# Cross-attention in two layers on one core: constants written into PSUM ahead of the products, g spread by a block transpose and two transfers, new orders on the engines

## What is computed

```python
# layer 0                                      # layer 1, on the x of layer 0
Q = x @ Wq + bq; K = c @ Wk + bk               q = x @ Wq + bq; k = c @ Wk + bk
V = c @ Wv + bv                                v = c @ Wv + bv
weights = softmax(Q @ K.T * scale, axis=-1)    w = softmax(q @ k.T * scale, axis=1)   # over the queries
x = x + (weights @ V) @ Wo + bo                y = w @ v + x
                                               y = (y - mean) * rsqrt(var + eps) * gamma + beta
```

## Time and profile before

| | |
|---|---|
| median of 3 runs | 1249.71 us (1248.47 to 1250.39) |
| the profiled execution's own time | 1247.58 us |
| its span, first to last instruction | 1245.8 us |
| busy PE | 1206.5 us, 97% |
| busy DVE | 892.8 us, 72% |
| busy ACT | 699.2 us, 56% |
| busy POOL | 926.9 us, 74% |
| the transfer engines' mean busy share | 5 to 6 tenths in most slices |
| mean granted TensorE clock | 0.989 of 2.4 GHz |

### The profile page before, as it was taken

One profiled execution on the slowest core, in us unless ns is written; L12 is line 12 of the kernel. 1 busy time (PEld: TensorE's weight loads), 2 busy tenths in 40 slices (PEclk: granted clock), 3 DMA queues, 4 the chain that ended last, 5 costly groups with the idle time before them and its releaser, 6 DMA issues.

```text
span 1245.8 us, 25385 instructions
## 1 busy us (share of the span) xinstructions
PE 1206.5 (97%) x8304; PEld 1116.0 (90%) x8304; DVE 892.8 (72%) x1874; ACT 699.2 (56%) x1545; POOL 926.9 (74%) x713
## 2 busy tenths in 40 slices
PE   6989999999999999999999999999999999999984
PEld 5779999999999999999999999999999999999973
DVE  1447777777777777777777777777777777777763
ACT  2436556555656655565665556565555656555542
POOL 2436778778777877887787788778778877877764
PEclk8999999999999999999999999999999999999998
DMA  8346556656656655665666566566656655665431
GB/s 329 104 142 210 175 201 222 196 188 210 227 168 207 222 195 185 219 219 170 206 222 195 184 216 221 175 202 220 197 182 219 219 180 199 219 196 186 153 119 51
DMA packets 121727, 241.36 MB, mean 194 GB/s; under 512 B 13920, under 2 KB 79456, under 8 KB 113120
## 3 DMA queue, kind: packets, MB, share of 16 engines
q1 hardware_dynamic: 120816, 240.18, 58.0%
q10 hardware_dynamic: 880, 0.79, 0.2%
HBM read 157.03 MB, written 83.89 MB: 193 GB/s over the span
## 4 chain that ended last, share of the span: by engine, by line
PE 92%; POOL 2%; DMA 2%; DVE 1%; issue 1%; ACT 1%; ACTq 0%; POOLq 0%; SPq 0%; DVEq 0%
PE bank L275 85%; PE bank L392 2%; PE bank L365 2%; DMA beta_b<-in_beta 1%; PE bank L344 1%; PE bank L402 1%; PE bank L408 1%; POOL PT_lo L915 0%; POOL Y L963 0%; DVE stats L802 0%; POOL yT_lo L915 0%; POOL Y L966 0%; PE bank L421 0%; ACT Y L603 0%; POOL rstd L953 0%
## 5 line engine op out<-in xcount | busy, mean ns | idle before, releaser
L915 POOL TENSOR_TENSOR PT_lo<-PT_raw,PT_hi 128x512 fp32r<-128x512 f32 x64 | 82.6, 1291 | 192.6 <-ACT PT_hi L482 192.6
L603 ACT ACTIVATE Y<-R,nmr,rstd 128x512 f32<-128x512 f32 x128 | 97.5, 809 | 184.5 <-POOL nmr L955 184.5
L915 POOL TENSOR_TENSOR xT_lo<-IN,xT_hi 128x1024 fp32r<-128x1024 f32 x64 | 154.2, 2409 | 24.7 <-ACT xT_hi L482 24.7
L915 POOL TENSOR_TENSOR yT_lo<-yT_raw,yT_hi 128x1024 fp32r<-128x1024 f32 x64 | 154.1, 2407 | 21.4 <-ACT yT_hi L482 21.4
L963 POOL TENSOR_TENSOR Y<-Y,gamma_b 128x512 f32<-128x512 f32 x128 | 162.8, 1294 | 3.7 <-ACT Y L603 3.7
L966 POOL TENSOR_TENSOR Y<-Y,beta_b 128x512 f32<-128x512 f32 x128 | 163.4, 1299 | 0.0
L275 PE MATMUL bank<-yT_hi,A_hi 128*128 128x256 f32 x512 | 144.5, 282 | 4.9 <-POOL yT_lo L915 4.9
L275 PE MATMUL bank<-yT_lo,A_hi 128*128 128x256 f32 x512 | 144.9, 283 | 0.0
L275 PE MATMUL bank<-yT_hi,A_lo 128*128 128x256 f32 x512 | 144.7, 283 | 0.0
L275 PE MATMUL bank<-xT_hi,A_hi 128*128 128x256 f32 x512 | 144.1, 281 | 0.0
L275 PE MATMUL bank<-xT_lo,A_hi 128*128 128x256 f32 x512 | 144.0, 281 | 0.0
(11 more groups left out here) (116 smaller groups left out, 4199.0 us busy)
## 6 DMA issues: line engine op xcount, KB each, us to landing
IN<-in_packed SPq DMA_DIRECT2D x64, 1024.0 KB, 5.7
R<-in_x SPq DMA_DIRECT2D x64, 512.0 KB, 6.3
y_dram<-y_blk SPq DMA_DIRECT2D x256, 128.0 KB, 2.4
yT_raw<-y_dram SPq DMA_DIRECT2D x64, 512.0 KB, 3.6
out<-Y SPq DMA_DIRECT2D x64, 512.0 KB, 3.5
E_dram<-E_blk SPq DMA_DIRECT2D x256, 64.0 KB, 1.8
PT_raw<-E_dram SPq DMA_DIRECT2D x64, 256.0 KB, 2.7
WqT_s<-in_WqT SPq DMA_DIRECT2D x2, 1024.0 KB, 11.5
```

The lines of the kernel that those rows point to most:

```text
L603: nc.scalar.activation(Y[n.k % 2][:, q, :], R[n.k % 4][:, q, :], ACT.Identity, bias=nmr[:, q:q + 1], scale=rstd[:, q:q + 1]).then_inc(Y_se ...
L915: return nc.gpsimd.tensor_tensor(dst, src, fp(hi), ALU.subtract)
```

## The change

What the changed kernel does:

- **out.** `out_seed_` on ACT writes c1 * Z0 into the bank before the products of `out_`, which then add to it (`seeded=True`: no matmul starts a new sum). c1 is a row made in the setup from bo and bv. The banks of `out_` and of `pred_` are no longer the same.
- **S1 and g.** `g_` and `gT_` are gone. `dot` writes g into the first column of a block of 32, `g_blocks` on DVE transposes the blocks, SP writes 256 numbers to DRAM (`write_g`) and reads them back to all 128 partitions (`read_g`), `S1_seed_` on ACT copies them into the bank of S1, and the products add to it. The addition on DVE is gone.
- **s.** `w_low_sum` on DVE adds the two halves of w_lo; `s_` is 3 matmuls with a tile of ones. `s_h` and `s_l` are gone. `s_columns` on DVE brings s into columns by four transposes, each on 32 partitions, 64 numbers a partition. s shares its bank with u, so `u_` of the next body waits for `s_columns`.
- **pred.** `pred_seed_` on DVE writes bv*s + x1 into the bank; the two bias matmuls and `x2` are gone. `moments` and `normalise` read the bank.
- **Orders.** The bodies of all five engines have new orders, and the setup of PE, ACT, DVE and SP too. In it one matmul with the tile of ones is new, and POOL's constants are gone.

```diff
-        g_bank = s_bank = bank[0]
+        out_bank = (bank[0], bank[3])
         Pc_bank = v_bank = bank[1]
-        u_bank = bank[2]
-        g1_b = bank[3]
+        u_bank = s_bank = bank[2]
         S0_bank = wc_bank = bank[4]
         S1_bank = bank[5]
-        out_bank = pred_bank = bank[6:8]
+        pred_bank = bank[6:8]
...
-                first(sp, Y_set, n.count(2, 1, back=4))
+                first(sp, pred_seed, n.count(2, 1, back=4))
...
+            def write_g(n):
+                if not n.there():
+                    return
+                sp.wait_ge(g_blk_set, n.count())
+                sp.dma_start(g_dram.rearrange("q i t -> i q t"), g_blk[0:P:32, :, :]).then_inc(g_out, 16)
+            def read_g(n):
+                if not n.there():
+                    return
+                sp.wait_ge(g_out, n.count(16, 15))
+                sp.dma_start(gT[:, 0, :], g_dram.rearrange("(a q) i t -> a (q i t)", a=1).to_broadcast([P, S])
+                             ).then_inc(g_in, 16)
...
             def body(r):
+                write_g(r.plus(1))
+                load_x(r.plus(2))
                 load_IN(r.plus(5))
-                load_x(r.plus(2))
-                store(r.plus(-2))
+                read_g(r.plus(1))
                 move_E0(r.plus(3))
                 move_y(r.plus(2))
+                store(r.plus(-2))
...
-            def product(dst, stat, mov, k, first=True):
+            def product(dst, stat, mov, k, seeded=False):
                 for t in range(k):
                     for n, (a, b) in enumerate(((0, 0), (0, 1), (1, 0))):
-                        last = nc.tensor.matmul(dst, stat(a, t), mov(b, t), start=(first and t == 0 and n == 0),
-                                                stop=(t == k - 1 and n == 2))
+                        last = nc.tensor.matmul(dst, stat(a, t), mov(b, t), start=(not seeded and t == 0 and n == 0),
+                                                stop=(t == k - 1 and n == 2), skip_group_check=seeded)
                 return last
...
+                first(pe, s_set, n.count(back=4))
...
-                first(pe, x1_set, n.count(2, q, back=1))
-                first(pe, x2_set, n.count(2, q, back=3))
+                pe.wait_ge(out_seed, n.count(2, q))
                 product(out_bank[q][:, :], lambda a, t: PcT[a][:, t, q * P:(q + 1) * P],
-                        lambda b, t: Bv[b][:, t, :], LT).then_inc(out_full, 1)
+                        lambda b, t: Bv[b][:, t, :], LT, seeded=True).then_inc(out_full, 1)
...
-            def g_(n):
-                if not n.there():
-                    return
-                pe.wait_ge(g_set, n.count(2, 1))
-                first(pe, s_lo, n.count(back=1))
-                for q in range(ST):
-                    last = nc.tensor.transpose(g_bank[:, q * P:(q + 1) * P],
-                                               gcol[n.k % 2][:, q:q + 1].to_broadcast([P, P]), ident[:, :])
-                last.then_inc(g_full, 1)
-
             def S1_(n):
                 if not n.there():
                     return
                 pe.wait_ge(v_lo, n.count())
-                first(pe, w_lo, n.count(back=1))
+                pe.wait_ge(S1_seed, n.count())
                 for m in range(ST):
                     last = product(cols(S1_bank, m), lambda a, t: cTs[n.k % 4][a][:, t, m * P:(m + 1) * P],
-                                   lambda b, t: vT[b][:, t, :], LT)
+                                   lambda b, t: vT[b][:, t, :], LT, seeded=True)
                 last.then_inc(S1_full, 1)
             def s_(n):
                 if not n.there():
                     return
-                pe.wait_ge(w_lo, n.count())
-                pe.wait_ge(gT_set, n.count())
-                for t in range(ST):
-                    for b in range(2):
-                        last = nc.tensor.matmul(s_bank[:, 0:S], pick[:, :], w[b][:, t, :],
-                                                start=(t == 0 and b == 0), stop=(t == ST - 1 and b == 1))
+                if n.plus(3).there():
+                    pe.wait_ge(u_lo, n.plus(3).count(2, 1))
+                else:
+                    pe.wait_ge(s_set, n.count(back=1))
+                pe.wait_ge(w_los_set, n.count())
+                for t, part in enumerate((w[0][:, 0, :], w[0][:, 1, :], w_los[:, :])):
+                    last = nc.tensor.matmul(s_bank[:, 0:S], ones[:, :], part, start=(t == 0), stop=(t == 2))
                 last.then_inc(s_full, 1)
...
-                    pe.wait_ge(s_lo, n.count())
                     pe.wait_ge(wc_lo, n.count())
-                if n.plus(2).there():
-                    pe.wait_ge(x1_set, n.plus(2).count(2, q))
-                else:
-                    pe.wait_ge(x2_set, n.count(2, q, back=1))
-                dst = pred_bank[q][:, :]
-                nc.tensor.matmul(dst, srow[:, q * P:(q + 1) * P], bvK[:, :], start=True, stop=False)
-                product(dst, lambda a, t: wcT[a][:, t, q * P:(q + 1) * P], lambda b, t: V1[b][:, t, :], LT,
-                        first=False).then_inc(pred_full, 1)
+                pe.wait_ge(pred_seed, n.count(2, q))
+                product(pred_bank[q][:, :], lambda a, t: wcT[a][:, t, q * P:(q + 1) * P],
+                        lambda b, t: V1[b][:, t, :], LT, seeded=True).then_inc(pred_full, 1)
...
+            over_h(bank[7][:, :], wide(1), Wo0_s)
...
+            pe.wait_ge(su_lo, 7)
+            A_half(bank[5], WqT1_s, WkT1_s, 1)
...
-            over_h(bank[5][:, :], wide(1), Wo0_s)
+            pe.wait_ge(su_lo, 9)
+            pe.wait_ge(ones_set, 2)
+            nc.tensor.matmul(S1_bank[:, :], ones[:, :], Bv[0][:, 0, :], start=True, stop=True).then_inc(su_full, 1)
             v_(Seq(0))
-            pe.wait_ge(const_set, 2)
-            pe.wait_ge(pick_set, 2)
-            pe.wait_ge(su_lo, 11)
             def body(r, u=True):
                 if u:
                     u_(r.plus(3))
+                S1_(r)
                 Pc_(r.plus(2))
-                g_(r)
-                S1_(r)
                 S0_(r.plus(3))
                 pred_(r.plus(-1), 0)
                 pred_(r.plus(-1), 1)
...
-            def gT_(n):
-                if not n.there():
-                    return
-                act.wait_ge(g_full, n.count())
-                first(act, S1_sum, n.count(back=1))
-                copy(gT[:, 0, :], g_bank[:, 0:S]).then_inc(gT_set, 1)
+            def S1_seed_(n):
+                if not n.there():
+                    return
+                act.wait_ge(g_in, n.count(16, 15))
+                first(act, w_lo, n.count(back=1))
+                copy(S1_bank[:, :].rearrange("p (a b) -> p a b", a=ST), gT[:, :, :].to_broadcast([P, ST, S])
+                     ).then_inc(S1_seed, 1)
+            def out_seed_(n):
+                if not n.there():
+                    return
+                act.wait_ge(E0_set, n.count())
+                for q in range(ST):
+                    first(act, x1_set, n.count(2, q, back=1))
+                    copy(out_bank[q][:, :], c1_b[:, :], scale=Z0[:, q:q + 1]).then_inc(out_seed, 1)
...
-            def s_h(n):
-                if not n.there():
-                    return
-                act.wait_ge(s_full, n.count())
-                first(act, pred_full, n.count(2, 1, back=1))
-                copy(srow[0:96, :], s_bank[0:96, 0:S]).then_inc(s_hi, 1)
-
...
-                    nc.scalar.activation(Y[n.k % 2][:, q, :], R[n.k % 4][:, q, :], ACT.Identity,
+                    nc.scalar.activation(Y[n.k % 2][:, q, :], pred_bank[q][:, :], ACT.Identity,
...
             def body(r, prefix=True):
                 if prefix:
                     wc_h(r.plus(-1))
+                    u_h(r.plus(3))
                     C_h(r.plus(3))
-                    u_h(r.plus(3))
+                xT_h(r.plus(4))
+                if prefix:
+                    out_seed_(r.plus(2))
+                exps1(r)
                 Pc_h(r.plus(2))
-                gT_(r)
+                w_h(r)
                 yT_h(r.plus(1))
+                exps0(r.plus(3))
+                S1_seed_(r.plus(1))
+                v_h(r.plus(1))
                 cT_h(r.plus(4))
-                xT_h(r.plus(4))
-                exps0(r.plus(3))
-                exps1(r)
-                w_h(r)
                 normalise(r.plus(-1))
-                v_h(r.plus(1))
-                s_h(r)
                 PT_h(r.plus(3))
...
-                first(dve, g_set, n.count(2, q, back=1))
-                first(dve, g_full, n.count(back=2))
                 nc.vector.scalar_tensor_tensor(junk[q][:, :], R[n.k % 4][:, q, :], 1.0, g1_b[:, :], ALU.mult,
-                                               ALU.mult, accum_out=gcol[n.k % 2][:, q:q + 1]).then_inc(g_set, 1)
+                                               ALU.mult, accum_out=gcol[:, q, 0:1]).then_inc(g_set, 1)
+            def g_blocks(n):
+                if not n.there():
+                    return
```

(77 more changed lines are left out.)

110 lines of the change are left out of this document (49 added, 61 removed).

## The result

The changed kernel takes 1400.7 us (median of 4 runs, 1400.3 to 1401.1), the kernel before 1249.6 (4 runs): a ratio of 1.121, 95% interval 1.1195 to 1.1224. I had forecast 1245, range 1203 to 1264. The profiled execution took 1400.27 us, its span is 1398.5.

The account below looks back on a forecast made before the run. PE bound the kernel before at 18.15 us a body; after, a loop through s_columns of 10.62 + 7.46 = 18.08 would, gaining 4.2 us. With setup +4 and tail -3.9 that is -4.1 from 1249.7: about 1245, range 1203 to 1264.

Parts of the forecast that it names:

- All totals remain below 17.3.: Busy totals of ACT, DVE and POOL per body after the change: all stay below 17.3 us.
- New is w_low_sum: ... like srow's 0.42 less the overlap, 0.34.: DVE leg of the loop: the new sum of the w_lo halves, 256 columns, priced at 0.34 us.
- the walk: Loop from u's first matmul through ACT, DVE and s_columns back to u: 10.62 + 7.46 = 18.08 us a round.
- The ends: Outside the regular rounds: setup +4 us (0 to +8), tail -3.9 us.
- the loop that binds: u of the next body waits for s_columns on DVE: 18.08 us a round against PE's 17.34.
- the two out seeds: On ACT ahead of exps1: 1.22 us together, between 1.04 and 1.52.
- four transposes held apart: s_columns on DVE: 4 x 0.23 and three gaps of 0.03, 1.03 us.
- 0.22 a body for g's transposes: On PE: dropping the two transposes of g spares 0.22 us a body.
- (a): Rival: transposes of s overlap (0.6), seeds cost a plain copy (1.04); round 17.5, gain 37 us, 1212; chance 0.22.
- (b): Rival: PE stays the bound at 17.34, the loop 0.74 shorter; gain 49 us, 1201; chance 0.12.
- (c): Rival: transposes of s cost 0.42 + 0.03 each; round 18.85, 42 us longer, 1292; chance 0.13.
- (d): Rival: g lands late, S1_seed holds up ACT; decides from 17.3, at 18.3 period 19.15, 1310; chance 0.05.

Follow-up runs that it names:

- a_nolo: Changed kernel with GpSimd's gamma and beta products and its low parts of x and c (xT_lo, cT_lo) cut to 2 columns: 1258.0 us, ratio 1.0072.
- a_nofin: Changed kernel with GpSimd's products with gamma and beta cut to 2 columns: 1314.8 us, ratio 1.0519 to the kernel before.
- a_bank_s4: Changed kernel with dot and pred seed reading v's PSUM bank, w_low_sum removed and s made by four matmuls: 1268.2 us, ratio 1.0162.
- the fastest one: Kernel before with g by block transpose and two transfers, loads first on SP, y(1)'s moves ahead of g's in setup: 1239.2 us, ratio 0.9919.
- b_g2: Kernel before with g by block transpose and two transfers, SP's loads first, read_g between E0's write and read: 1243.7 us, ratio 0.9955.
- b_g: Kernel before with g by block transpose and two transfers, write_g at the head of SP's list: 1390.8 us, ratio 1.1118.

## Why the prediction was wrong

- **"All totals remain below 17.3."** This step failed. I counted DVE's operations by their old durations and priced two new ones by rows of others, without asking where their inputs lie. DVE's total is 18.3 us a round. The dot, the same operation as before, went from 680 to 1757 ns because its input left PSUM. Run a_nolo shows the same list at 18.26 a round once most of GpSimd's work is out of the way, with DVE at 14.8.
- **"New is w_low_sum: ... like srow's 0.42 less the overlap, 0.34."** The mis-sized term: 1.4 us, 1.06 too short. srow's addition has one input in a bank; `w_low_sum` has both in SBUF. 0.42 is right where GpSimd is idle (425 ns in a_nofin). A warning stood in the trace of before: V_lo in the setup, a subtraction with both inputs in SBUF, took 2214 ns for 1024 columns, while the transpose of as many takes 1.25 us; it had started 0.17 us behind a C_lo of GpSimd of 1.29.
- **What the walk left out.** The seeds of pred and the second dot were left out of the walk, as no part of the loop. At 2.7 us the dot came into it in 48 of 59 rounds, by the reciprocal behind it that ACT waits for: 0.98 a round in the mean. And the walk has PE at its higher level throughout; in nine rounds it fell to the lower one, 1.1 to 1.5 us each, which the next round gave back.
- **The ends.** Setup +8.9 for my +4: PE reached S1 at 89.40 for my 87.7, 4.5 later than before; the other 4.4 came between there and the first regular u_h, partly at the lower level of the clock, and I did not divide them. In a_nolo the loop begins no earlier (108.01), so it wasn't GpSimd. Tail +7.0 for −3.9: it is −2.1 in a_bank_s4, with GpSimd's work whole, and −4.7 in a_nolo, where the last products with gamma and beta are cut too. So most of the miss is the stretch; whether −3.9 was right stays open.
- **Right:** the loop that binds, and its closing wait (u for the last transpose of s); the whole walk in the first round, where nothing of GpSimd held these legs up, 18.07 for 18.08; the two out seeds, whose follower starts 1.23 after them for 1.22; four transposes held apart, 1.01 us for 1.03; 0.22 a body for g's transposes. Of the rivals, (a) and (b) need a loop that was never this short in the changed kernel (and (a)'s own terms give 17.47, 0.68 a round and 41 us, where I wrote 0.62 and 37); (c) did not occur, each transpose takes 0.24; nor did (d), though narrowly: g is there 16.7 us behind u's first matmul (717.43 to 734.12) for my 14.7, and behind it ACT still waits 2.1 for `normalise`.
- **Open:** I did not try the change with its dot reading a PSUM bank and the right values: out and pred have taken the last free bank. So which of its other parts would pay was measured only in the kernel before, and there only for g and for s in three matmuls.

## What to carry to other kernels

When a tensor moves from PSUM to SBUF, price again every VectorE instruction that reads it, and look what GpSimd is doing at that time: a sum of busy times holds neither. A transfer that waits for a late result belongs behind the loads on its queue, since everything issued after it goes late; in the kernel before, that order was worth ten times the operation it served. When a new wait closes a loop through an engine that was slack, each operation ahead of it on that engine costs in every round.

## What the runs showed of the hardware that I had not expected

- An instruction of VectorE with two inputs in SBUF does next to nothing while an instruction of GpSimd that started first is running: the dot takes 0.65 to 0.69 us alone, up to 2.76 beside xT_lo, and ends 0.53 to 0.56 behind GpSimd's instruction in each of the six kernels that have it in SBUF; with an input in PSUM it takes 0.67 to 0.69 in every kernel.
- One with a single small input in SBUF (128x2, `ve`) is held too, 178 to 736 ns. The Trainium skill's page named above, SBUF — State Buffer, section "SBUF: two separate sides", has the lock for a two-port mode as well; that this instruction ran in one no row shows.
- GpSimd is held as well when it comes second: xT_lo took 2.85 us instead of 2.41 behind a dot. In the mean it loses less, its product with gamma 1378 ns in the changed kernel and 1299 in the fastest one, where VectorE has few such instructions.
- 64 KB land in 1.8 us or in 6.1, by what stands just ahead of them on SP's queue (b_g2, b_g).
- PE's clock fell behind nine of 48 waits of 1.9 to 2.4 us, and not always behind the longest of them.
